# Four edits to a two-layer transformer kernel: opening, lists of experts, first rows written, turned value product

## What is computed

```python
# layer 0 and layer 1, with their own weights and conditions
mod = silu(c) @ wmod                      # sa, ca, ga, sb, cb, gb; ca and cb get +1
h = layernorm(x) * (1 + ca) + sa
x = x + ga * attention(h)
h = layernorm(x) * (1 + cb) + sb
x = x + gb * feed_forward(h)
```

## Time and profile before

| | us |
|---|---|
| median of 3 runs (lowest, highest) | 1327.55 (1325.54, 1330.53) |
| the profiled execution's own time | 1333.13 |
| its span, first to last instruction | 1331.0 |
| attention 0 / router / experts / attention 1 / feed-forward 1 | 624.4 / 90.8 / 258.4 / 211.8 / 145.6 |
| busy over the span: PE, DVE, ACT, POOL | 1001.3, 809.2, 611.0, 424.9 |

### The profile page before, as it was taken

One profiled execution on the slowest core, in us unless ns is written; L12 is line 12 of the kernel. 1 busy time (PEld: TensorE's weight loads), 2 busy tenths in 40 slices (PEclk: granted clock), 3 DMA queues, 4 the chain that ended last, 5 costly groups with the idle time before them and its releaser, 6 DMA issues. The chain is left out here.

```text
span 1331.0 us, 24972 instructions
## 1 busy us (share of the span) xinstructions
PE 1001.3 (75%) x8508; PEld 684.6 (51%) x8508; DVE 809.2 (61%) x1812; ACT 611.0 (46%) x2042; POOL 424.9 (32%) x312
## 2 busy tenths in 40 slices
PE   5679899898989898986612487776428989877765
PEld 2446556565656565655602355453316666655554
DVE  5755867666666757563656515112235889749995
ACT  2465776767575757563201132311115555543422
POOL 2432333323232423221000568787710121200221
PEclk8699999999999999997555789888759999978867
DMA  6563343434343434340401124346320000000000
GB/s 194 139 178 97 87 111 99 110 95 112 80 113 87 111 98 112 97 102 17 123 0 60 29 52 74 61 58 149 28 67 1 1 1 1 1 0 9 16 16 24
DMA packets 89872, 93.61 MB, mean 70 GB/s; under 512 B 18768, under 2 KB 63296, under 8 KB 89808
## 3 DMA queue, kind: packets, MB, share of 16 engines
q1 hardware_dynamic: 78544, 84.12, 24.1%
q0 software_dynamic: 11264, 8.66, 4.8%
HBM read 24.36 MB, written 10.70 MB: 26 GB/s over the span
## 5 line engine op out<-in xcount | busy, mean ns | idle before, releaser
L797 POOL TENSOR_TENSOR qk_cos<-qk_raw,const 128x512 f32<-128x512 f32 x128 | 181.0, 1415 | 356.2 <-ACT qk_raw L562 356.2
L548 ACT ACTIVATE prob<-psS,neg_max 128x96 f32<-128x96 f32 x512 | 167.5, 342 | 75.0 <-DVE neg_max L643 74.8
L415 PE MATMUL psQ<-a_xnT,weights 128*128 128x512 f32 x246 | 141.8, 659 | 17.3 <-ACT v_tok L567 16.6
L523 PEld LDWEIGHTS psO<-probT,v_windows 96*64 96x64 f32 x2048 | 72.8, 142 | 122.9 <-ACT probT L620 97.8
L1463 POOL DMA_INDIRECT sums<-ex_y,ex_index x64 | 102.4, 1601 | 36.3 <-issue 18.6
L523 PE MATMUL psO<-probT,v_windows 96*64 96x64 f32 x2048 | 90.9, 233 | 25.7 <-ACT probT L620 25.3
L658 DVE TENSOR_TENSOR qk_roped<-qk_cos,qk_swapped 128x512 f32<-128x512 f32 x128 | 105.9, 827 | 5.1 <-DVE qk_swapped L649 4.6
L1453 POOL DMA_INDIRECT ex_rows<-rows,ex_index x64 | 67.0, 1046 | 129.4 <-DMA ex_index<-lists 110.2
L548 ACT ACTIVATION_READ_ACCUMULATOR prob<-psS,neg_max 128x1 f32 x512 | 106.0, 207 | 0.0
L1398 ACT ACTIVATE ex_hidden<-ex_psH,ex_b 128x512 f32<-128x512 f32 x64 | 43.5, 687 | 125.2 <-DVE ex_index L1527 53.3
L620 ACT COPY probT<-psT 96x512 f32<-96x512 f32 x128 | 74.8, 584 | 55.4 <-PE psT L503 55.3
(11 more groups left out here) (317 smaller groups left out, 1964.0 us busy)
## 6 DMA issues: line engine op xcount, KB each, us to landing
qk_swapped<-qk_raw SPq DMA_DIRECT2D x512, 64.0 KB, 2.0
v_windows<-v_tok SPq DMA_DIRECT2D x32, 384.0 KB, 4.4
v_windows<-v_tok SPq DMA_DIRECT2D x32, 256.0 KB, 3.6
mod<-mod_rows SPq DMA_DIRECT2D x12, 512.0 KB, 6.2
ex_w<-in_L_ffn_W SPq DMA_DIRECT2D x16, 256.0 KB
v_windows<-v_tok SPq DMA_DIRECT2D x32, 96.0 KB, 2.1
rows<-rt_h SPq DMA_DIRECT2D x8, 256.0 KB, 2.4
sums<-rt_zeros SPq DMA_DIRECT2D x8, 256.0 KB, 2.7
```

The source lines that it names most:

```text
L415: last = nc.tensor.matmul(bank, k.wqkvT[:, col:col + P], xnT[:, :], start=True, stop=True)
L523: ins = nc.tensor.matmul(psO[D * j:D * j + D, u % 2, i * P + a * HALF:i * P + (a + 1) * HALF], vw[:, par, a, t, hd], probT[:, 2 * j + i, a ...
L548: last = nc.scalar.activation(prob[:, s, 2 * j + i, :], psS[:, s, j, i * KW:(i + 1) * KW], ACT.Exp, bias=nmax[:, s, 2 * j + i:2 * j + i + ...
L797: nc.gpsimd.tensor_tensor(rcos[:, half, :], raw[:, half, :], k.const[:, K_COS:K_COS + T], ALU.mult).then_inc(cos_done, 1)
```

## The change

1. Opening. `Modulation` uses other banks: its product for the first two rows goes to psQ alone and signals first; the copy of the turned silu (`turned`) comes before DVE's measuring of sequence 0; `normed(0)` comes ahead of the second gate. The block that measured sequences 1 to 7 is gone; in unit 0 of each sequence's body DVE measures the next sequence and finishes its norm (`finish_one`), and POOL takes its root (`root_one`, 4 columns; before, `root_rest`, 28 columns).
2. Lists. `GROUP` is 2 in place of 4, so there are four groups of two experts; `low`, `low_of` and `high` have two buffers; the list of a group is taken after the next group's `low`.
3. Expert 0 writes its rows to `sums` (`bypass`) in place of adding them.
4. Attention 1. The value product is turned: weights `v` (64 columns), moving `probT` (128 columns), both heads of a tile into psO's two halves of partitions. So `oT` comes without `turn_o`; the scaling by 1/sum moves behind the output projection, which is made head by head into psQ and psY: ACT scales head 0 (`scale_y`), DVE adds head 1 scaled (`residual`). Both norms' normalising moves from DVE to ACT (`normalise_act`, with a bias -mean x rstd that POOL makes). The loop goes by tiles, scores are made two tiles ahead, and the FP4 steps are spread otherwise.

```diff
-GROUP = P // SPLIT
+GROUP = 2
 GROUPS = E0 // GROUP
+LISTED = GROUP * SPLIT
...
     def multiply(self, pe):
-        nc.tensor.matmul(self.banks[0][0:B, 0:half], self.siT[:, :], self.w[:, 0:half], start=True, stop=True)
-        nc.tensor.matmul(self.banks[1][0:B, 0:2 * C], self.siT[:, :], self.w[:, half:MODS * C], start=True, stop=True).then_inc(self.multiplied, 1)
+        nc.tensor.matmul(self.banks[0][0:B, 0:2 * C], self.siT[:, :], self.w[:, 0:2 * C], start=True, stop=True).then_inc(self.multiplied, 1)
+        nc.tensor.matmul(self.banks[1][0:B, 0:4 * C], self.siT[:, :], self.w[:, 2 * C:MODS * C], start=True, stop=True).then_inc(self.multiplied, 1)
...
+    def normalise_act(self, act, b, out):
+        act.wait_ge(self.rstd_ready, 2 * b + 2)
...
+        for t in range(TILES):
+            last = self.nc.scalar.activation(out[:, t, :], k.x[:, b, t, :], ACT.Identity, bias=bias[:, b, t:t + 1],
+                                             scale=rstd[:, b, t:t + 1])
...
             mod.silu(dve)
+            mod.turned(dve)
             dve.wait_ge(ld_x[0], 16)
...
             mod.finish_gate(dve, GA)
+            normed(0)
             mod.finish_gate(dve, GB)
-            normed(0)
...
-            take_sixth(5)
-            for i, (lo, hi) in enumerate(X_PARTS[1:]):
-                dve.wait_ge(ld_x[1 + i], 16)
-                for b in range(lo, hi):
-                    measure(nc, k, own, b)
-            dve.wait_ge(own.sem, own.n)
-            norm.finish(dve, own, TILES)
             for half in range(HALVES):
                 rope(0, 0, half, sines(0, 0, half))
+                if half == 0:
+                    take_sixth(5)
...
+                        if u == 0:
...
+                            measure(nc, k, own, b + 1)
+                            dve.wait_ge(own.sem, own.base + own.n)
+                            norm.finish_one(dve, own, b + 1)
...
+                    if u == 0 and not last:
+                        norm.root_one(pool, b + 1)
...
-                                                 y[:, par, n, :], None, compute_op=ALU.add).then_inc(scattered[par], 16)
+                                                 y[:, par, n, :], None, compute_op=ALU.bypass if written else ALU.add).then_inc(scattered[par], 16)
...
+            for g in range(GROUPS):
+                buf = g % 2
+                wait(dve, weighed, 2 * (g - 1))
+                one_hot(low[:, buf, :, :, :], 1, g, slice(0, NT)).then_inc(lows, 1)
+                if g > 0:
+                    take_list(g - 1)
...
+            def apply(b, par, t):
+                n = b * TILES + t
+                pe.wait_ge(probT_ready, H1 * (n + 1))
+                wait(pe, oT_ready, n)
...
+                for c in range(TILES):
+                    for j in range(H1):
+                        hd = slice(j * D, (j + 1) * D)
+                        last = nc.tensor.matmul(psO[hd, 0:P], v[:, par, c, hd], probT[:, j, c, :],
+                                                start=(c == 0), stop=(c == TILES - 1), skip_group_check=True)
...
+                    for j, bank in enumerate((psQ, psY)):
+                        rows = slice(D * j, D * j + D)
+                        last = nc.tensor.matmul(bank[:, t * C:(t + 1) * C], oT[rows, par, t * P:(t + 1) * P], k.w1oT[rows, :],
+                                                start=(t == 0), stop=True, skip_group_check=True)
...
+            def normalise2(b):
+                wait(act, quantised2, b)
+                norm2.normalise_act(act, b, h2[:, :, :]).then_inc(normed2, 1)
...
+                    copy_oT(b, par, t)
+                    if t == 0 and next1:
+                        piece(b + 1, 1 - par, 1)
+                    if t == 1 and next2:
+                        normalise(b + 2)
+                    if t == 3:
+                        if next2:
+                            copy_hT(b + 2)
+                        if 0 <= b - 1 < EARLY:
+                            normalise2(b - 1)
...
+                    if u in (3, 4, 5):
+                        next(added, None)
                     if u == 5 and 0 <= b - 1 < EARLY:
                         finish2(b - 1)
-                    next(steps, None)
-                    if u in (1, 6):
+                    for _ in range((0, 0, 2, 2, 0, 1, 3, 2)[u]):
                         next(steps, None)
...
+                    if u == 6 and next2:
+                        modulate(b + 2)
+                next(steps, None)
```

More of the change, by code:

```diff
@@ L194, in finish @@
     def finish(self, dve):
+        self.turned(dve)
         self.finish_shift(dve)
@@ L1334, in _ @@
                         pe.wait_ge(highs, 2 * g + 1 + t // (NT // 2))
[L1335 removed]
+                    last = nc.tensor.matmul(psL[g % 2][0:LISTED, 0:2 * LISTED], high[:, g % 2, t, :, :], low_of[:, g % 2, :, t, :, :],
                                             start=(t == 0), stop=(t == NT - 1))
@@ L1381, in _ @@
                 act.wait_ge(lows, g + 1)
-                nc.scalar.activation(low_of[:, 0, :, :, :].rearrange("p t e l -> p (t e l)"),
-                                     low[:, :, :, :].rearrange("p t e l -> p (t e l)"), ACT.Copy,
+                wait(act, listed, g - 1)
+                nc.scalar.activation(low_of[:, g % 2, 0, :, :, :].rearrange("p t e l -> p (t e l)"),
+                                     low[:, g % 2, :, :, :].rearrange("p t e l -> p (t e l)"), ACT.Copy,
                                      scale=k.const[:, K_TOKEN:K_TOKEN + 1]).then_inc(weighed, 1)
@@ L1458, in scatter @@
                 wait(pool, scattered[1 - par], 16 * SLOTS * (turn + par))
+                written = isinstance(e, int) and e == 0
                 for n in range(SLOTS):
@@ L1519, in _ @@
                 last.then_inc(ids_ready, 1)
+            for g in range(GROUPS):
[4 more added lines that the diff above has]
+                    take_list(g - 1)
+                dve.wait_ge(lows, g + 1)
+                nc.vector.tensor_tensor(low_of[:, buf, 1, :, :, :].rearrange("p t e l -> p t (e l)"),
+                                        low[:, buf, :, :, :].rearrange("p t e l -> p t (e l)"),
+                                        iota[:, :].unsqueeze(2).to_broadcast([P, NT, LISTED]), ALU.mult).then_inc(weighed, 1)
+                for half in range(2):
+                    one_hot(high[:, buf, :, :, :], 0, g, slice(half * NT // 2, (half + 1) * NT // 2)).then_inc(highs, 1)
+            take_list(GROUPS - 1)
             def keep(e, par, turn):
@@ new lines, in body @@
+                for t in range(TILES):
+                    turn_prob(b, t, 0)
+                    if t + 2 < TILES or next1:
+                        pe.wait_ge(exp_done, (b * TILES + t + 1) * H1)
+                        score(b, par, t + 2)
+                    turn_prob(b, t, 1)
+                    if t in (0, 2) and next1:
+                        project(b + 1, t)
+                    if t == 1 and not first:
+                        out_project(b - 1, 1 - par)
+                    apply(b, par, t)
+                    if t == 0 and next1:
+                        project(b + 1, 1)
+                    if t == 3 and next2:
+                        turn_x(b + 2)
@@ L1697, in piece, with scale_y, normalise @@
                 nc.scalar.copy(out, psQ[:, :]).then_inc(piece_out, 1)
+            def scale_y(b):
+                act.wait_ge(y_ready, b + 1)
+                act.wait_ge(rsum_ready, b + 1)
+                wait(act, y_read, b)
+                for t in range(TILES):
+                    last = nc.scalar.activation(yhead[:, t, :], psQ[:, t * C:(t + 1) * C], ACT.Copy, scale=rsum[:, 0, t:t + 1])
+                last.then_inc(y_scaled, 1)
+            def normalise(b):
+                wait(act, x_turned, b)
+                norm.normalise_act(act, b, h[:, :, :]).then_inc(normed1, 1)
+            def normalise2(b):
+                wait(act, quantised2, b)
+                norm2.normalise_act(act, b, h2[:, :, :]).then_inc(normed2, 1)
             def copy_oT(b, par, t):
-                act.wait_ge(o_turned, b * TILES + t + 1)
-                nc.scalar.copy(oT[:, par, t * P:(t + 1) * P], psOT[:, 0:P]).then_inc(oT_ready, 1)
+                act.wait_ge(applied, b * TILES + t + 1)
+                wait(act, y_ready, b - 1)
+                nc.scalar.copy(oT[:, par, t * P:(t + 1) * P], psO[:, 0:P]).then_inc(oT_ready, 1)
+            normalise(0)
             copy_hT(0)
+            normalise(1)
             for m in range(3):
```

283 lines of the change are left out of this document (140 added, 143 removed).

## The result

| | before | after |
|---|---|---|
| median of 13 runs each | 1327.3 us | 1336.4 us |
| profiled execution, span | 1331.0 us | 1334.6 us |

What follows compares the result with a forecast made beforehand. GpSimd was taken to bound the experts, no single engine attention 1, mostly PE attention 0's loop. Terms -5.1 + 7.0 - 6.0 - 4.9 - 13.7 = -22.7 us gave a forecast of 1305 us, range 1287 to 1320.

Steps and rivals of the forecast that it cites:

- Opening, -5.1: Attention 0's opening: earlier first projection and SP swaps bring the last rotation to 35.1 from 40.2, saving 5.1 us.
- Norms in the loop, +7.0: Attention 0's loop: of 2.1 us added DVE work, 1.05 hidden and 1.0 exposed, over seven sequences +7.0 us.
- The bound of +14.7: Attention 0's loop: rival with nothing of the norms hidden, +14.7 us in place of +7.0, giving 1313; chance 0.08.
- Lists, -6.0: Expert stage: first list stored earlier, gathers run beside DVE's work, the eighth landing at 752.5 instead of 758.79, saving 6.0 us.
- Written rows, -4.9: Expert stage: scatter 0's eight DMAs, writing instead of adding, take 0.94 rather than 1.56 us each, saving 4.9 us.
- Attention 1, work: Attention 1: product 1.05 us; PE about 17, DVE 17, ACT 16.7 us busy a sequence; period 19 or 20 by busy time.
- The serial product and its 1344 us: Attention 1: rival in which the turned product runs in series at 2.1 us, period 26.4, total 1344 us; chance 0.09.
- Attention 1, the cycle, -13.7: Attention 1: a dependency cycle sets the period at 21.7 against 23.14 us; with edges and end, -13.7 us.
- the ring: Attention 1: ACT's second norm waits for DVE's FP4 steps, DVE's addition for ACT's scaling; 21.7 us round.
- The rivals: Attention 1 period 19.8 (0.20); written rows save nothing (0.14); gathers starve (0.07); norms fully exposed (0.08); product in series (0.09).

## Why the prediction was wrong

- **Opening, -5.1: right**, step by step, with SP's queue as the new limit.
- **Norms in the loop, +7.0: this step failed.** Its two terms were sound: 1.05 us hidden and 1.0 exposed, and 0.97 was measured on the spot. Wrong was the step from there to seven times 1.0, that the delay costs itself and no more. "DVE has no slack up to 295" was written there, and that the cosines queue behind the root, but what a later VectorE would meet was put at nothing. It met GpSimd's cosines (2.0 us), and the later copies left TensorE idle for 2.35 us, behind which its clock fell (1.35 us). The clue was in the earlier trace rows: four normalisings of 1.60 us where the opening had 1.11. I took that for the price of the loop's computed addresses. With the cosines cut to one column, the same four in the same loop take 1.11 us; the 1.60 was already a meeting with a cosine. The bound of +14.7 was no bound for that reason: it counted VectorE's work only. Measured: 4.33 us a sequence, some 21.5 us in this phase.
- **Lists, -6.0: right in mechanism and nearly in size.** 5.5 us at scatter 0 on the chip without gaps. The gathers did get through beside VectorE's work: most of the first eight took 1.4 to 2.0 us, two 0.95. Expert 0's keep came 38.9 us into the phase and not 37.3, for VectorE issued its last list ahead of it.
- **Written rows, -4.9: right in size** (4.7 for the pieces, 4.7 to 5.0 in the stage). Of both terms together 8.9 us of 10.9 came, 1.4 being lost behind.
- **Attention 1, work: right but for VectorE.** The product takes 1.09 us, TensorE 17.5 at full clock (17), ScalarE 17.2 (16.7), VectorE 18.7, where 17 was 1.7 too low. The serial product and its 1344 us did not come.
- **Attention 1, the cycle, -13.7: the ring is real, one term was too small, and the clock was missing.** ScalarE's norm takes 1.65 us and not 1.2, which makes 22.15; with the clock held up 22.29 was measured, and the phase gained 9.9 us. The idle time that the ring puts on TensorE (2.61 us) then cost 1.6 us a sequence, and the gain was 3.5. Of the 3.8 us between 13.7 and 9.9, the norm's 0.45 in each of the four middle sequences makes about half; where the rest lies stays open.
- **The rivals.** None was the case. All of them priced the work or the waiting; none priced what the waiting does to TensorE. The rows at 155.6 us of the kernel before, and its 74.71 us for one sequence of 70.75, were enough to see that one such meeting can cost 4 us (the later runs show 1.06, 2.4 and 4.1 us, by what the clock does). The rival on the other side should have been this one.

The Trainium skill (TensorE: Matmul & The Clock Gate, "HAM oscillation — how this bites in real kernels") says that a wait in each round of a loop can bring TensorE back to half its clock in each round. The traces agree: in the changed kernel's profile 0.79 in the stretch of unit 3 shown and the same period in every looped sequence, 0.93 over a sequence of attention 1, and 1.00 in both once the gap was filled.

## What to carry to other kernels

In a loop whose TensorE is nearly always busy, a new wait of 2 us is not worth 2 us: look at what the granted clock did the last time that the engine stood idle as long, and add that. Work moved onto an engine shifts everything behind it, so list what the shifted operations will run beside, and not only what they wait for. A duration that is longer in one place than in another, as the normalising's 1.60 us, is worth a look at what ran beside it. The static first iteration was a place for work that was exposed in every turn, and a second buffer cut a ring through three engines.

## What was unexpected in the hardware

- TensorE's clock fell behind idle times of 1.63 to 2.61 us, but not behind all. Behind 2.35 us it fell in 28 of 30 looped sequences; with the root left out, the same 1.95 us were followed by a lower clock in one sequence (period 77.4) and by 1.00 in another (72.8). In the 40 looped sequences without an idle time over 1.1 us (seven profiles) it fell once, behind 0.85 us. So the periods of such a loop come in several sizes. Filling the gap with twelve matmuls that nobody reads shortened the loop.
- A VectorE operation that starts just behind a GpSimd one takes more than twice as long: sine 1.76 and 1.79 us (0.68 alone), normalising 2.56 (1.11 alone; 1.60 in the kernel before, beside part of a cosine). The Trainium skill (SBUF — State Buffer, "Who interferes with whom") says that a VectorE instruction with two SBUF inputs contends with GpSimd's reads and that issue order decides who waits. The sines agree: 0.03 us behind a cosine of 1.26 us, one took 1.1 us longer.
- In all six profiles of the first two sets (both kernels and four variants), TensorE's stream of expert 0's down projection had gaps of up to 2.5 us for which the profile shows no cause, and the eight profiles of the later sets, from two other chips, show none. The expert stage took 258.4 us in the kernel before and 248.2 to 250.7 in the changed one where they stand, and 248.7 and 239.1 to 239.8 (rows written) where they don't. What they are stays open.
